# One core, sixteen blocks, an order worked out when the program is built: longer hand-overs and a margin in the planner's rules

## What is computed

```
x = L0_attn_a_x
x = x + scan(norm(x));      x = x + experts(norm(x))       # blocks 0, 1
x = x + linear_attn(norm(x)); x = x + experts(norm(x))     # blocks 2, 3
x = x + gla(norm(x));       x = x + local_attn(norm(x))    # blocks 4, 5
x = x + latent_attn(norm(x)); x = x + local_attn(norm(x))  # blocks 6, 7
x = x + conv_scan(norm(x)); x = x + swiglu_experts(norm(x))# blocks 8, 9
x = x + masked_attn(norm(x)); x = x + swiglu_experts(...)  # blocks 10, 11
x = x + block_attn(norm(x)); x = x + slots(norm(x))        # blocks 12, 13
x = x + global_and_local_gqa(norm(x)); x = x + slots(...)  # blocks 14, 15
```

## Time and profile before

| | |
|---|---|
| median of 3 runs | 3631.7 us |
| the profiled execution's own time | 3608.04 us |
| its span, first to last instruction | 3606.7 us |
| mean granted TensorE clock | 0.935 |
| instructions | 52,771 |
| PE matmul, weight load | 84%, 51% busy |
| DVE, ACT, POOL | 66%, 61%, 39% busy |
| HBM traffic | 75 GB/s over the span |

### The profile page before, as it was taken

The page is one execution under the profiler, slowest core; times in us unless marked ns, Lnnn a source line. Parts: engine busy times, 40 slices in busy tenths (PEclk is TensorE's granted clock), DMA queues, the critical chain, the costliest instruction groups (busy, mean ns, idle before and its releaser), DMA issues. The chain is left out here.

```text
span 3606.7 us, 52771 instructions
## 1 busy us (share of the span) xinstructions
PE 3038.5 (84%) x18500; PEld 1822.3 (51%) x18500; DVE 2381.2 (66%) x6084; ACT 2202.3 (61%) x4827; POOL 1394.7 (39%) x1308
## 2 busy tenths in 40 slices
PE   3678887999889999889999887878788787789987
PEld 0244556657545555444555434546545476554344
DVE  2778774675777776667768889965444444655764
ACT  2456554534466777667767766947656566466874
POOL 1445554444345554224646554643220222100320
PEclk9889998999999999999999999989988999789997
DMA  6343343113200010220101123543532254321420
GB/s 228 97 128 111 105 112 109 57 44 100 68 14 1 1 32 8 76 52 15 51 1 33 33 81 100 166 130 103 135 82 61 61 178 112 99 46 31 92 52 10
DMA packets 216897, 271.96 MB, mean 75 GB/s; under 512 B 39544, under 2 KB 154936, under 8 KB 214584
## 3 DMA queue, kind: packets, MB, share of 16 engines
q1 hardware_dynamic: 192312, 191.11, 18.7%
q0 software_dynamic: 24320, 77.47, 7.2%
HBM read 217.02 MB, written 54.00 MB: 75 GB/s over the span
## 5 line engine op out<-in xcount | busy, mean ns | idle before, releaser
L371 ACT ACTIVATE scratch<-psum 128x512 f32<-128x512 f32 (+6 forms) x1780 | 828.0, 497 | 808.2 <-PE psum L327 578.7
L327 PE MATMUL psum<-scratch 128*128 128x128 f32 (+19 forms) x8016 | 942.9, 324 | 110.2 <-ACT scratch L371 51.0
L463 POOL TENSOR_TENSOR scratch<-scratch 128x512 f32<-128x512 f32 (+3 forms) x536 | 614.7, 1162 | 697.0 <-DVE scratch L424 216.0
L327 PEld LDWEIGHTS psum<-scratch 128*32 128x32 f32 (+9 forms) x8016 | 601.2, 148 | 476.9 <-issue 224.4
L327 PE MATMUL psum<-scratch,w_constants 128*128 128x512 f32 (+2 forms) x848 | 453.5, 635 | 131.8 <-DVE scratch L393 110.2
L371 ACT ACTIVATE scratch<-scratch 128x512 f32<-128x512 f32 (+8 forms) x856 | 395.8, 469 | 246.5 <-DVE scratch L393 167.1
L363 ACT ACT_TABLE_LOAD x357 | 458.0, 1283 | 23.5 <-DVE scratch L393 9.1
L393 DVE TENSOR_TENSOR scratch<-psum,scratch 128x512 f32<-128x512 f32 (+2 forms) x696 | 376.2, 551 | 115.0 <-ACT scratch L371 83.3
L343 PE MATMUL psum<-w_constants,scratch 128*128 128x128 f32 (+2 forms) x1880 | 316.3, 289 | 61.0 <-ACT scratch L371 22.4
L407 DVE TENSOR_TENSOR_SCAN psum<-psum,scratch 128x512 f32<-128x512 f32 x256 | 309.3, 1222 | 77.1 <-ACT psum L371 63.5
L371 ACT ACTIVATE psum<-scratch 128x255 f32<-128x255 f32 (+1 forms) x528 | 221.4, 456 | 193.2 <-DVE scratch L393 188.2
(11 more groups left out here) (108 smaller groups left out, 4016.0 us busy)
## 6 DMA issues: line engine op xcount, KB each, us to landing
scratch<-b_and_c_out SPq DMA_DIRECT2D x256, 256.0 KB
slots_out<-scratch SPq DMA_DIRECT2D x112, 128.0 KB
q_stack<-scratch SPq DMA_DIRECT2D x72, 192.0 KB, 2.4
scratch<-q_out SPq DMA_DIRECT2D x96, 96.0 KB
scratch<-slots_in SPq DMA_DIRECT2D x16, 512.0 KB
q_out<-scratch SPq DMA_DIRECT2D x40, 192.0 KB, 3.1
scratch<-slots_in SPq DMA_DIRECT2D x16, 448.0 KB
scratch<-q_stack SPq DMA_DIRECT2D x24, 288.0 KB
```

Source lines behind the costliest of these rows:

```text
L327: return self.engine.matmul(out, lhsT, rhs, start=start, stop=stop, **kw)
L371: return self.engine.activation(out, src, function, **kw)
L463: return self.engine.tensor_tensor(out, a, b, op)
```

## The change

Four things are edited. `LAG` is 50 ns longer on PE, ACT, DVE and POOL, and stays on SP. A new `MARGIN` of 100 ns (0 on SP) is added to the time at which a waiting step counts as ready, in the rank alone; the planned clock goes on from `at + LAG` without it. `keep_clock` is called for every PE step with a key, up to `at + LAG`, where it was called up to the rank; it still does nothing where that time has passed. And the weights of `L1_gla` start at column 2048 of `w_early` instead of right behind those of `L0_linear` (1252 + 782 = column 2034): columns 1024 to 2047 are spare room of stream 1.

```
-    LAG = 30
+    LAG, MARGIN = 30, 100
 class Tensor(Engine):
-    LAG, DRAIN, COLD, STEP, SPAN, ENOUGH, WANTED = 55, 160, 50, 13, 3413.3, 0.37, 0.5
+    LAG, DRAIN, COLD, STEP, SPAN, ENOUGH, WANTED = 105, 160, 50, 13, 3413.3, 0.37, 0.5
 class Scalar(Engine):
-    LAG, LN_EXP, LN_EXP_TABLE, SWITCH = 36, (ACT.Ln, ACT.Exp), 6, 1300
+    LAG, LN_EXP, LN_EXP_TABLE, SWITCH = 86, (ACT.Ln, ACT.Exp), 6, 1300
 class Vector(Engine):
-    LAG, DRAIN = 33, 80
+    LAG, DRAIN = 83, 80
 class Pool(Engine):
-    LAG, INDIRECT = 80, 1250
+    LAG, INDIRECT = 130, 1250
 class Sync(Engine):
+    MARGIN = 0
     LAG, ISSUE = 27, 450
 class Core:
+    def rank(self, p, e):
+
+        at = self.value[p.key][2] + e.LAG + e.MARGIN if p.key is not None else e.free
+        return max(e.free, at) + e.delay(p.function), at
     def run(self, programs):
-                e = self.engines[p.engine]
-                at = self.value[p.key][2] + e.LAG if p.key is not None else e.free
-                rank = max(e.free, at) + e.delay(p.function), at
+                rank = self.rank(p, self.engines[p.engine])
-            rank, p = best
-            if p.engine == "pe" and rank[0] > self.engines["pe"].free:
-                self.keep_clock(rank[0], going)
+            p = best[1]
             e = self.engines[p.engine]
+            if p.engine == "pe" and p.key is not None:
+                self.keep_clock(self.value[p.key][2] + e.LAG, going)
-FROM = {"L1_attn": 3 * SPARE, "L2_scan": 4 * SPARE}
+FROM = {"L1_gla": 2 * SPARE, "L1_attn": 3 * SPARE, "L2_scan": 4 * SPARE}
```

## The result

The change makes the kernel 2.5% slower: a median of 3722.9 us (3712.8 to 3739.2, 4 runs) against 3632.8 us, a ratio of 1.025 with a 95% interval of 1.021 to 1.029. The forecast was 3662 us with a range up to 3715. The side was right, the size was not: +90 us where +30 was forecast.

The account below looks back on a forecast made before the run. PE was taken as near its limit, 84% busy, with streams feeding each other in rings. Terms of 22 - 5 + 12 + 0 = +29 us, with 0.8 us +30, on 3631.7 gave 3662 us, range 3590 to 3715.

Parts of the forecast that it names:

- Term 3: End of PE's order: stream 3 alone for eight groups of block 14 and block 15, +12 us, between -2 and +23.
- stream 2's share moved to where PE works at 0.9: Block 15: stream 2's work moves into a shared stretch and one stream's chain sets the length, costed at nothing.
- the lone tail at a low clock: Rival: stream 3's lone groups at clock 0.59, +36 us, and all 35 loads count, +45: 3713 us; chance 0.12.
- Term 1: ACT: 35 more table loads of 1.283 us, partly on the chain, +22 us, between 0 and 44.9.
- The figure of 2.66 us for a switch of table: Rival on ACT: draining after each load doubles the cost of the loads, +52 us in all, 3684 us; chance 0.03.
- Term 2: ACT: giving up waiting sooner starts steps that switch table up to 0.15 us earlier, -5 us, between -5 and 0.
- The interleaving for hand-overs that don't occur: Planner: the new 105 ns hand-over on PE is about twice the real one, so streams are interleaved for untrue hand-overs.
- Term 4: All queues: everything else in the order is dealt anew, taken at 0, bounds 89 us either way.
- What would show it: Signs: 392 loads, chain share above 12%, lone last stretch of 90 to 110 us, PE's waits for ACT above 159 us.
- the 25 that were to refute term 3: Sign at the tail: the lone-tail term is wrong if stream 3's eight lone groups take no longer than 25 us.

Follow-up runs that it names:

- change_again: The change itself, unedited, run again beside the kernel before on another chip: 3608.7 us against 3531.1, ratio 1.021.
- before_again: The kernel before, unedited, run for a profile on a chip of the experiments: span 3522.7 us.
- before_tail_open: The kernel before with stream 3's steps taken 3 us later in the choice from block 12 on: 3593.6 us against 3528.3, ratio 1.020.
- tail_closed: The change with stream 3's steps taken 3 us earlier in the choice from block 12 on: 3552.7 us, ratio 1.007 to the kernel before.
- loads_357: The kernel before, same order, with one more table load ahead of each of its 357: 3922.0 us against 3531.1.
- lag1: The kernel before with each LAG of PE, ACT, DVE and POOL 1 ns longer: 3590.9 us, ratio 1.017.
- lag10: The kernel before with each LAG of PE, ACT, DVE and POOL 10 ns longer: 3536.7 us, ratio 1.001; without table loads 3494.7 us.

## Why the prediction was right in its side and wrong in its size

**Term 3, the lone tail, is the step that failed.** It was taken at +12 us with bounds of -2 and +23. The readings put it at 41 to 46 us (the rate of matmuls), 48 and 50 us (tail closed, with and without loads), and 65 to 69 us (tail opened in before). The prediction even named what would be seen, "a last stretch of 90 to 110 us with stream 3 alone and PE busy some 65%": it was 95.2 us, and 61.77 / 95.2 = 65%.

For that stretch itself its price was nearly right. Take the two profiles of change_again and before_again, and 7.2 matmuls a microsecond as the full pace. The 45 us ahead of block 15 hold 179 matmuls, worth 25 us: 20 us lost, where 12 was forecast. The eight groups took 37 us in the first profile of the change, and the forecast comes to 22 + 12 = 34; what no term held is the end of block 14, the last 6 us of that stretch. Block 15 was costed "at nothing", because one stream's chain sets its length, and that came out at 2 us: the last 51.9 us hold 92 matmuls, worth 13, and before the last 56.7 us hold 140, worth 19, so 39 us are lost now and 37 were lost before.

What failed is the sentence on the work that leaves the end: "stream 2's share moved to where PE works at 0.9". It does not work at 0.9 there. In the 96 us ahead of the lone stretch PE executes 499 matmuls, 5.2 a microsecond, busy 81.12 of 96 us at a clock of 0.81, because with stream 3 behind the other three run out one after another. At 7.2 a microsecond 27 us are lost there. Before, the 136 us ahead of the last 56.7 hold 692 + 372 - 140 = 924 matmuls, worth 128 us, and 8 are lost. These 19 us were in no term, and 20 + 2 + 19 = 41. That it is the lagging stream and not the loads shows in the same 96 us of before_tail_open, which hold 499 matmuls too, and of tail_closed, which hold 731. The prediction priced the stretch with one stream left and took what lies ahead of it as full.

The rival "the lone tail at a low clock" came nearest with 3713 us, and by luck. It had the clock right, 0.59 forecast and 0.53 measured, but its sum holds +36 for the groups, which took 37 us and not the 58 that this means, and +45 for the loads; both are too high, and make up for what it had at nothing as well.

**Term 1, the table loads**, forecast at +22 us within 0 and 44.9, came out at 13 us: 77 us between the two orders with loads, 64 without, a difference that is uncertain by about its own size. It does not refute 22. The share on the chain, 64%, was neither price: it was too low for a load that is added (85%, loads_357) and too high for those that the planner had laid out (0.24 / 1.283 = 19%). The chain says how much of the loads lay on it, not what an order made for other loads would do.

The figure of 2.66 us for a switch of table (the Trainium skill, "ScalarE: Activation LUTs", What ACT_TABLE_LOAD costs) is not borne out by loads_357 either. Its 357 loads more, all but 14 of another table than the one loaded, cost 1.10 us each, and no drain shows between the two loads of a pair.

**Term 2** left no trace that could be told from the rest. The explanation of the loads behind it fell: "The order bears that out: 392 table loads instead of 357" is weak evidence for a shorter patience, since LAG + 1, which shortens it by 1 ns, gives 399.

**"The interleaving for hand-overs that don't occur"** is not needed for the loss. With hand-overs as true as before, lag1 is 1.7% slower, and with 10 ns too many, lag10 is not slower. Whether 50 ns too many cost something by themselves, no run shows.

**Term 4, the shuffle at zero**: 77 less about 50 for the tail and 13 for the loads leaves some 14 us, which is 0.4% and within what the readings of the tail disagree by. But it is not zero in general: lag10's order is 50 us worse without loads, with nothing in its end to show for it. Its bound of 89 us either way was fair, and it belonged into the upper end of the range more than it was: the range ended 8 us short of the measured time.

**What would show it**: 392 loads and 44 us more of ACT, as said. "Their share of the chain above 12%" was wrong: 11.1% over the stretch from 2269 us on. PE's waits for ACT rose to 167 us and its idle time to 640 us, as said. The lone stretch was as described, and its eight groups took 37 us, longer than the 25 that were to refute term 3.

How far the tail is shown: three edits move only the choice between streams from block 12 on, and time follows the lone stretch in both directions, with and without loads. They re-deal the queues of blocks 12 to 15 as well, so each carries some luck of its own; 41 to 69 us is the spread. Why stream 3 falls behind in the change stays open. At the end of block 7 it is already 166 us behind the next stream, against 118 before; from there to the end the gap closes to 95 us, and before to 17. MARGIN and LAG each by itself leave it 45 and 63 us alone.

## What to carry to other kernels

Where several streams share engines, read first when each of them ends: the time in which one works alone was paid at 2.8 matmuls a microsecond instead of 7.2 and at half the clock, and the 96 us ahead of it at 5.2. Preferring the stream that lags took 1.4% off the change and 0.4% off the kernel before. To price such an end, count the work in equal stretches back from the end of both orders, until they hold the same; the stretch with one stream left is only part of it. And test a planner's setting against its neighbours: 1 ns in LAG moved this kernel by 1.7%, so a gain or a loss of that size after an edit of its rules is no verdict on the rule.

## What the hardware showed that was not expected

One instruction had two prices in one queue. A table load added to a fixed order cost 1.10 us of its 1.283, and one removed from it gave back 0.24; that the neighbours in the other queues stay where the planner put them would explain it, but is not shown. And chips differ: the kernel before has medians of 3633 us on the first and 3528 to 3531 us on the three others, 3% apart. The profiled executions have mean granted clocks of 0.935 and 0.945, but that is not the reason: executions at 0.925 to 0.935 on the three others took 3520 to 3549 us. The reason stays open. The change cost 90 us on the first and 78 on another, with intervals of the ratio (1.021 to 1.029, 1.018 to 1.023) that overlap.
